# q, k and v of the second layer from four fp32r products in one PSUM bank, with a newly chosen order of all queues

## The reference

```
mod = silu(c) @ Wa + ba; sh_msa, sc_msa, g_msa, sh_mlp, sc_mlp, g_mlp = split(mod, 6)
h = layernorm(x) * (1 + sc_msa) + sh_msa
q, k, v = h @ Wq, h @ Wk, h @ Wv                  # 144 -> 3 x 144
w = softmax(q k^T / 3)                            # layer 1: causal; layer 0: full
x = x + g_msa * ((w v) @ Wp + bp)
h = layernorm(x) * (1 + sc_mlp) + sh_mlp
x = x + g_mlp * (act(h @ W1 + b1) @ W2 + b2)      # gelu in layer 0, silu in layer 1
```

## Time and profile before

| | |
|---|---|
| median of 3 runs | 292.33 us (292.04 to 294.12) |
| profiled execution | 292.45 us |
| its span, first to last instruction | 290.6 us |
| mean granted clock of TensorE | 0.988 |
| busy: TensorE, its weight loads, VectorE, ScalarE, GpSimd | 272.4, 157.0, 214.4, 198.2, 102.2 us |

### The profile page before, as it was taken

How to read it: one execution, slowest core, us unless ns; L and a number is a source line. 1 busy time by engine, 2 the same in 40 slices (tenths; PEclk the granted TensorE clock), 3 DMA queues, 4 the chain that set the end, 5 groups by cost and what they waited for, 6 DMA issues and landing times.

```text
span 290.6 us, 6567 instructions
## 1 busy us (share of the span) xinstructions
PE 272.4 (94%) x2418; PEld 157.0 (54%) x2418; DVE 214.4 (74%) x435; ACT 198.2 (68%) x357; POOL 102.2 (35%) x217
## 2 busy tenths in 40 slices
PE   8998889999999999999999989999799999899986
PEld 3685533434443634555636657665555455477576
DVE  7478999987677699996219997875655869943583
ACT  2163757778888698987884678476688776893271
POOL 6859084580005410001093120237824324311100
PEclk9998999999999999999999979999999999999999
DMA  5750000000000000000000000000000000001001
GB/s 144 215 139 1 2 0 0 3 0 2 0 2 0 2 0 2 2 2 0 0 2 2 0 2 2 2 0 3 0 2 2 2 1 2 3 0 33 10 2 42
DMA packets 5587, 4.60 MB, mean 16 GB/s; under 512 B 762, under 2 KB 5121, under 8 KB 5556
## 3 DMA queue, kind: packets, MB, share of 16 engines
q1 hardware_dynamic: 5556, 4.18, 5.2%
HBM read 3.59 MB, written 0.59 MB: 14 GB/s over the span
## 4 chain that ended last, share of the span: by engine, by line
PE 66%; DVE 15%; POOL 7%; issue 5%; ACT 5%; POOLq 0%; ACTq 0%; DVEq 0%
PE OB L1379 14%; DVE negm L1165 8%; PE banks L1358 7%; PE banks L1314 7%; PE banks L1331 7%; PE banks L1419 5%; PE banks L1286 3%; ACT probs L993 3%; PE banks L1287 2%; PE banks L1386 2%; PE banks L1216 2%; PE banks L1224 2%; POOL rowsT L876 2%; POOL rowsT L872 2%; PE banks L1277 2%
## 5 line engine op out<-in xcount | busy, mean ns | idle before, releaser
L1165 DVE TENSOR_REDUCE negm<-banks 128x2 f32<-128x1024 f32 (+2 forms) x112 | 124.4, 1141 | 29.2 <-PE banks L1342 19.1
L993 ACT ACTIVATE probs<-banks 128x1024 f32<-128x1024 f32 (+1 forms) x112 | 106.6, 966 | 27.6 <-PE banks L1358 25.4
L1379 PE MATMUL OB<-probs,V 128*10 128x512 f32 (+3 forms) x512 | 55.8, 515 | 0.4 <-POOL probs L906 0.4
L1331 PE MATMUL banks<-KS,QS 54*128 54x512 bf16 (+3 forms) x256 | 41.4, 346 | 2.7 <-DVE negm L1165 1.5
L1358 PE MATMUL banks<-QS,KS 56*128 56x512 bf16 (+3 forms) x256 | 39.5, 341 | 3.3 <-DVE negm L1165 1.2
L906 POOL TENSOR_SCALAR_AFFINE_SELECT probs<-probs 128x512 f32<-128x512 f32 x32 | 20.6, 646 | 54.4 <-ACT probs L993 54.4
L1314 PE MATMUL banks<-identb,rowsT 128*128 128x128 bf16 x384 | 29.7, 225 | 2.5 <-POOL rowsT L876 1.1
L1331 PEld LDWEIGHTS banks<-KS,QS 54*128 54x128 bf16 x256 | 11.8, 93 | 34.0 <-issue 11.9
L1314 PEld LDWEIGHTS banks<-identb,rowsT 128*128 128x128 bf16 x384 | 22.8, 100 | 12.2 <-issue 8.6
L1358 PEld LDWEIGHTS banks<-QS,KS 56*128 56x128 bf16 x256 | 10.9, 93 | 25.9 <-issue 12.3
L826 POOL TENSOR_TENSOR rstd<-veps,half 128x2 f32<-128x2 f32 (+1 forms) x14 | 10.4, 745 | 39.0 <-DVE veps L1095 38.9
(11 more groups left out here) (128 smaller groups left out, 463.1 us busy)
## 6 DMA issues: line engine op xcount, KB each, us to landing
X<-in_x SPq DMA_DIRECT2D x2, 288.0 KB, 3.3
out<-X SPq DMA_DIRECT2D x8, 72.0 KB, 1.6
xh<-in_L_cond_W_ada SPq DMA_DIRECT2D x2, 216.0 KB
xh<-in_L_cond_Wa SPq DMA_DIRECT2D x1, 432.0 KB
at<-in_L_cond_W_fc SPq DMA_DIRECT2D x1, 288.0 KB
xh<-in_L_cond_W SPq DMA_DIRECT2D x1, 288.0 KB
w_fc<-in_L_cond_W_fc SPq DMA_DIRECT2D x1, 288.0 KB
w_fc<-in_L_cond_W SPq DMA_DIRECT2D x1, 288.0 KB
```

Source lines behind the costliest of these rows:

```text
L993: nc.scalar.activation(e, s, ACT.Exp, scale=SCALE).then_inc(bank_free[BANK[item]], 1)
L1165: nc.vector.tensor_reduce(m, s, AX.X, ALU.max, negate=True).then_inc(bank_free[BANK[item]], 1)
L1331: ins = nc.tensor.matmul(o[:, i * w:(i + 1) * w], QS[b][rows, h // 2 + pair, qt * P:(qt + 1) * P], KS[b][rows, h // 2 + pair, 0:w], start= ...
L1379: ins = nc.tensor.matmul(OB[CT * j:CT * j + VW, q0:T], V[b][:, kt, h + j, :], probs[:, kt % 2, j, q0:T], start=(kt == 0), stop=(kt == NT - 1))
```

## The change

It has two parts.

In layer 1 (`WIDE = (1,)`) the items `qk` make q, k and v together: four fp32r products of 432 columns for one token tile, in one bank. For this hT is split on VectorE as for fc1 (the same hT_p and hT_s), the layer's q, k and v weights are split on chip by a new item `qsplit` (three copies on ScalarE, two subtractions on GpSimd, one more clearing on GpSimd in the opening), and ScalarE copies v out of the same bank before it rounds q and k. The items `v` of layer 1 go. Layer 0 keeps its fp32 products.

The order is another one: `HASTE`, `READING` and `CALM` have new values, and a table `NUDGE` adds a number to the precedence of 98 single steps. `WINDOW`, which was 0, goes.

```diff
+WIDE = (1,)
+def has_parts(l, k):
+    return k == 1 or l in WIDE
...
-WEIGHTS = ([("acol", 0, 1), ("agate", 0, 0), ("agate", 0, 1), ("wsplit", 0, 1), ("wsplit", 1, 1),
+WEIGHTS = ([("acol", 0, 1), ("agate", 0, 0), ("agate", 0, 1), ("wsplit", 0, 1), ("wsplit", 1, 1), *(("qsplit", l, 0) for l in WIDE),
...
-            if k:
+            if has_parts(l, k):
                 add("side", "DVE", item, (1600 if r else 1070) * size + 130 * (size < 1), ("ACT", item))
...
-OTHERS, CALM = 3, 4
-HASTE = {'head': (0, -1000, 27000, 0), 'tail': (3000, 8000, -3000, 0), 'gather': (-1000, 0, 15000, 0), 'shift': (0, 8000, 0, 0)}
+OTHERS, CALM = 3, 5
+HASTE = {'head': (-3000, 20000, 20000, 43000), 'tail': (4000, 31000, -3000, 0), 'gather': (-3000, 0, 3000, 1000),
+         'shift': (0, -1000, 23000, 0)}
...
-READING = {'weights': 5000, 'side': 300000, 'strips': 20000, 'shift': 60000, 'gather': 300000}
+READING = {'weights': 60000, 'side': 20000, 'strips': 20000, 'shift': 300000, 'gather': 300000}
...
+NUDGE = {('ACT', 'qT', (0, 0)): 6000, ('PE', 'sT', 15): 28500, ('DVE', 'proj', (1, 0)): 5500, ('DVE', 'max', 4): -4000,
...
+    first = {(q[0], item): urgency[q[0], item] + haste(q[1], item) + reading(q[0], q[1], item)
+             + NUDGE.get(of_what(q[0], item), 0) for q, items in queues.items() for item in items}
...
+            for l in range(L):
+                if l in WIDE:
+                    nc.gpsimd.memset(w_q_s[l][:, :].bitcast(F32), 0.0)
...
+        def q_pieces(l):
+            s, r = w_q_s[l], w_qkv_r[l][0:R, :]
+            return [(w_qkv[l][:, :], w_q[l][0][:, :], w_q[l][1][:, :]), (r, s[0:R, :], s[64:64 + R, :])]
...
+                elif kind == "qsplit":                                  # GpSimd
+                    l, _ = args
+                    pool.wait_ge(high_q[l], 1)
+                    (whole, high, low), (whole_r, high_r, low_r) = q_pieces(l)
+                    link(nc.gpsimd.tensor_tensor(low, whole, high.bitcast(F32), ALU.subtract))
+                    nc.gpsimd.tensor_tensor(low_r, whole_r, high_r.bitcast(F32), ALU.subtract).then_inc(low_q[l], 1)
+                    pool.wait_ge(low_q[l], 1)
...
+                elif kind == "qsplit":                                  # ScalarE
+                    l, _ = args
+                    act.wait_ge(qkv_in[l], 96 if l else 48)
+                    act.wait_ge(filled, 1)
+                    for whole, high, low in q_pieces(l):
+                        nc.scalar.activation(high, whole, ACT.Copy)
+                    nc.scalar.activation(w_q_s[l][32:32 + R, :], w_qkv_r[l][0:R, :], ACT.Copy).then_inc(high_q[l], 1)
...
                     if l:
                         full(act, ("sT", (b + 1) * NG - 1))
+                    if l in WIDE:
+                        attended(act, (b + 1) * NG - 1, NT - 1)
+                        nc.scalar.activation(V[b][:, t, :, 0:D],
+                                             bank_of(item)[:, QK:3 * C].rearrange("p (h d) -> p h d", h=H), ACT.Copy)
                     nc.scalar.activation(slots(b, t, slice(0, 2), HIGH, slice(0, H)),
...
                 elif kind == "qk":                                      # TensorE
                     l, b, t = args
+                    if l in WIDE:
+                        pe.wait_ge(low_q[l], 1)
+                        pe.wait_ge(split, HTN[("hT", l, b, 0, 0, part_with(l, b, 0, t))])
+                        tok = slice(t * P, (t + 1) * P)
+                        o = bank[:, 0:3 * C]
+                        nc.tensor.matmul(o, hT_p[0][:, tok], w_q[l][0][:, :], start=True, stop=False)
+                        nc.tensor.matmul(o, hT_p[0][:, tok], w_q[l][1][:, :], start=False, stop=False)
+                        nc.tensor.matmul(o, hT_p[1][:, tok], w_q[l][0][:, :], start=False, stop=False)
+                        nc.tensor.matmul(o, hT_s[:, tok], w_q_s[l][:, :], start=False, stop=True).then_inc(filled_bank, 1)
+                        continue
```

More of the change, by code:

```diff
@@ L77, in head_items @@
 def head_items(l, b):
-    after = ([("split", l, b, 0)] if (l, b) == (0, 0) else []) + [("v", l, b, i) for i in range(2)]
+    after = ([("split", l, b, 0)] if (l, b) == (0, 0) else []) + ([] if l in WIDE else [("v", l, b, i) for i in range(2)])
     qk = [("qk", l, b, t) for t in range(NT)]
@@ L204, in steps @@
             add(stream, "POOL", item, 2900, ("ACT", item))
+        elif kind == "qsplit":
+            add(stream, "ACT", item, 1430, 26000)
+            add(stream, "POOL", item, 2300, ("ACT", item))
         elif kind == "stats":
@@ L221, in steps @@
             if rows and rows != item[1:4]:
-                before = [("DVE", ("hT", *rows, 0, parts(*rows)[-1])) if rows[2] else ("PE", ("v", *rows[:2], 1))]
+                before = [("DVE", ("hT", *rows, 0, parts(*rows)[-1])) if rows[2] else ("PE", last_of_head(*rows[:2]))]
             if r == 0 and s != 1:
@@ L312 @@
 WORK = {"pv": 0.87, "acol": 0.03, "agate": 0.42, "max": 0.75, "scores": 0.8, "hT": 0.62, "aT": 0.62}
-WINDOW = 0
 def reader_of(item):
@@ L336, in mode, with of_what @@
+def of_what(engine, item):
+    return engine, item[0], item[1] if item[0] in ("max", "scores", "msplit", "sT", "pv", "oT", "o", "tri") else item[1:3]
 def mode(item):
@@ L424, in plan @@
                     start = max(start, at_best)
-                mine_best.append((start, -urgency[engine, item] - haste(stream, item) - reading(engine, stream, item) - (STICK if engine == "PE" and mode(item) == last else 0), engine, stream, item, k))
+                mine_best.append((start, -first[engine, item] - (STICK if engine == "PE" and mode(item) == last else 0), engine, stream, item, k))
             if mine_best:
-                first = min(mine_best)[0]
-                chosen = min((c for c in mine_best if c[0] <= first + WINDOW), key=lambda c: c[1])
+                chosen = min(mine_best)
                 if best is None or chosen[0] < best[0]:
@@ L524, in two_block_kernel @@
         w_qkv_r = [sb(f"w_qkv_r{l}", [SR, 3 * C]) for l in range(L)]
+        w_q = {l: [sb(f"w_q{l}{i}", [P, 3 * C], F32R) for i in range(2)] for l in WIDE}
+        w_q_s = {l: sb(f"w_q_s{l}", [SR, 3 * C], F32R) for l in WIDE}
         w_fc1 = [[sb(f"w_fc1{l}{i}", [P, FF], F32R) for i in range(2)] for l in range(L)]
@@ L625, in two_block_kernel @@
         tri_ready = sem("tri_ready")
+        high_q = {l: sem(f"high_q{l}") for l in WIDE}
+        low_q = {l: sem(f"low_q{l}") for l in WIDE}
         pv_done = sem("pv_done")
@@ L643, in two_block_kernel @@
         GATE = ordinals(("gate",))
-        HTN = {item: n for n, item in enumerate((i for i in SIDE if i[0] == "hT" and i[3]), 1)}
+        HTN = {item: n for n, item in enumerate((i for i in SIDE if i[0] == "hT" and has_parts(i[1], i[3])), 1)}
         NORM_SETS = list(dict.fromkeys(i[1:4] for i in SIDE if i[0] == "norm"))
@@ L706, in rows_used @@
             else:
-                full(eng, ("v", l0, b0, 1))
+                full(eng, last_of_head(l0, b0))
         block = ctx.enter_context(nc.Block())
@@ L1375, in _ @@
                     if kt % 2 == 0 and g % NG == 0:
-                        released(pe, ("v", l, b, kt // 2))
+                        for t in range(kt, kt + 2):
+                            released(pe, v_from(l, b, t))
                     q0 = first_query(l, kt)
```

36 lines of the change are left out of this document (33 added, 3 removed), and 8 rows, old and new, of the table NUDGE.

## The result

The changed kernel takes 301.75 us (median of 4 runs, 301.54 to 305.3), the kernel before on the same chip 293.23 (4 runs). The ratio is 1.0325, with a 95% interval of 1.0281 to 1.0369: slower by 3.3%, where 285.3 was forecast with a range up to 293.5.

A forecast was written before the change was run, and what follows sets the result against it. TensorE was taken as the bound, with batch 1's layer-1 projection a latency in front of GpSimd. 292.45 - 5.7 (products) - 1.4 (order, chain cost recovered) = 285.3 us; range 278.5 to 293.5.

The forecast's parts named there:

- The port: Eight new two-input VectorE subtractions can hold GpSimd's selects about 0.3 us each; counted 0, bound +1 us.
- The order: New queue orders start batch 1's layer-1 head earlier, recover its chain cost and close a TensorE hole: -1.4 us.
- The products: TensorE, layer 1's q, k, v: 16 fp32r products a batch at 0.19 us replace 5.90 us of fp32; gain 5.7 us.
- Splitting hT: Layer 1's heads: five more VectorE instructions per half set, 7.2 us; batch 0 free, +1.1 us on batch 1's chain.
- Rival C: VectorE becomes the bound at layer seams and heads, where splits queue among reductions: 296 to 299.7 us, chance 0.13.
- Rival D: The wide product on TensorE takes four passes, not one: 304.3 us, chance 0.02.
- ScalarE: Four V copies of 144 columns a batch, near 0.24 us each, replace two: +0.1 us a batch, hidden outside batch 1's chain.
- Rounding the weights: Layer 1's weight split on ScalarE and GpSimd plus a GpSimd clearing in the opening: cost zero, 0.45 if a reader waits.

The follow-up runs named there:

- experiment 1: The changed kernel, but GpSimd begins gating batch 1's layer-0 weights only when VectorE's norm of batch 1 is done: 293.27 us, ratio to before 1.0012.
- Experiments 9 to 12: Wide products in before's order, 302.93 us; two fp32 products instead, 308.86; experiment 1 with first-half splits earlier, 296.08; with batch 1's second half earlier, 295.76.
- the exact old order: The kernel before with its order kept item by item and only layer 1's wide products, their hT splits and the weight split put in: 302.93 us, 1.0302.
- the fp32 twin: The kernel of the exact old order, with two fp32 products of 432 columns in place of the four fp32r, still waiting for the splits: 308.86 us, 1.0529.

## Why the prediction was wrong

**The port** is the step that failed. It priced the collision of VectorE and GpSimd for the eight new two-input subtractions against GpSimd's selects, at 0 with a bound of +1. For GpSimd that was right: the longest select after is 697 ns, 928 before. But the added instructions were held themselves. In the head of batch 1 in experiment 1 two of the first five start just after a select and take 0.70 and 0.85 us, where they take 0.28 and 0.42 otherwise:

```profile
190.09 0.64 POOL L992 TENSOR_SCALAR_AFFINE_SELECT probs<-probs 128x512 f32<-128x512 f32 x1 [1.17 <-ACT probs L1091]
190.16 0.70 DVE L1217 CAST hT_s<-hT_r 16x256 fp32r<-16x256 f32 x1
191.91 0.64 POOL L992 TENSOR_SCALAR_AFFINE_SELECT probs<-probs 128x512 f32<-128x512 f32 x1 [1.19 <-ACT probs L1091]
191.97 0.85 DVE L1223 TENSOR_TENSOR hT_p<-hT,hT_p 128x256 fp32r<-128x256 f32 x1
```

The trace of before had this direction too, beside the one of the earlier trace rows:

```profile
250.51 0.64 POOL L906 TENSOR_SCALAR_AFFINE_SELECT probs<-probs 128x512 f32<-128x512 f32 x1 [0.29 <-ACT probs L993]
250.53 0.77 DVE L1124 CAST hT_p<-hT 128x256 fp32r<-128x256 f32 x1
```

And the price asked only what the *added* instructions would meet. The order had moved old instructions: GpSimd's gating and weight split of batch 1 now stood beside a norm with one input, which nothing in the diff touches. There too VectorE waits, and the hold lasts for the series, not for an instruction: 5.3 us, 8.5 with what followed. The rule that I drew on (the Trainium skill, "SBUF — State Buffer", section "SBUF: two separate sides") names this pair too, a VectorE instruction in a mode with two ports against a GpSimd one; that the norm ran in that mode no run shows. The runs agree that the two exclude each other, and show a length that I did not price.

**The order**, priced at -1.4 us with +1.7 and new waits at worst, failed likewise. The stretch at half clock was on my list (+1.7), but the one that came was longer (0.52 and 0.50 over the 9 us from 36 to 45, in two kernels with the same hole); filling the hole gave back 3.3. And order and products don't add up. Wide products cost 9.7 us in the old order and the order 6.8 with the old products, both against before; together they cost 0.2 (293.27 - 293.12). The new order seems to fit the longer heads: it gets batch 1's second norm done at the same time (190.1 against 190.7), and with a head 4.5 us longer group 11's maxima are still at 206.9 in both. Why it does so was not tested step by step.

**The products** was right in mechanism and size: 0.20 us a product (0.19 taken), TensorE 5.3 us less busy (5.7), 6.5 and 5.9 us less time in two pairs of kernels that differ in them alone.

**Splitting hT** was mis-sized. The five instructions take what was said (0.28 to 0.42 us) when no select is beside them, but I took +1.1 us for batch 1's chain and nothing for batch 0, as if they ran as soon as hT was there. In experiment 1 ScalarE's hT is ready at 188.4 us, the splits start at 190.16, behind two row maxima and the second half's norm, and the first product at 192.97. Of these 2.81 us (190.16 to 192.97) 0.85 are the two holds above. In batch 0's head the first half waits likewise (hT ready at 133.35, splits at 135.72). The second half's splits start at once, at 195.94 and 140.67, but its transposes stand behind the products of the first. Measured from norm to qk: +3.1 us in batch 0 (9.7 against 6.6) and +4.5 in batch 1 (10.8 against 6.3).

**Rival C** said that splits queue among the reductions and that VectorE's shortage turns TensorE's gain into idle time. Experiments 9 to 12 show it in these orders. Its place (the heads, 188 to 206 us) was right; its price, 3.6 to 7.2 us above before, was low for the old order (9.7, though the products gained 6). In the new order the products did bring their gain (6.5 us), and the order's own 6.8 cancelled it; how much of that is room made for the longer heads no run separates. **Rival D** is out, 0.20 us a product. **ScalarE**: a V copy of 144 columns took 0.29 us (0.24 taken). **Rounding the weights**: GpSimd still idles 2.17 us ahead of the first rstd, as forecast. In the exact old order the opening was 2.2 us late (1.5 in the fp32 twin), with TensorE's clock at 0.64 (0.70) in 36 to 45 us, while `qsplit` stood among ScalarE's first items; I did not try it elsewhere, so that cause is only argued.

Without the collision the time would have been just inside the range (293.27 against 293.5), and that would have been luck, with the gain missing all the same. Two errors of one sign stand behind the difference of 16.5 us: 8.5 for the collision, and 8.0 for heads and order (293.27 - 285.3).

## What to carry to other kernels

When a change reorders queues, list for every long unbroken GpSimd series which VectorE instructions from SBUF to SBUF now fall beside it, old ones first, and let the series wait for those that TensorE needs. A cheaper product that needs a step on another engine is worth its gain only where that step is not queued: read the queue of that engine between the source and the product, not the step's duration. Test order and content apart, in all four combinations, since each may be slower alone and neutral together.

## What the runs showed of the hardware

- A VectorE tensor_scalar from SBUF to SBUF that met a back-to-back series on GpSimd was held until the first gap in it, 0.07 to 0.08 us, for 5.31, 5.96, 5.91, 5.90, 5.95 and 2.37 us in six kernels. A row maximum, which reads PSUM, took its usual 1.23 us beside the same series (at 27.58 us in after). With one select of 0.64 us beside them, casts and subtractions of hT took 0.32 to 0.48 us longer. The wait shows as the instruction's own duration; an engine that looks full (8.00 of 8 us with six instructions) may be held. GpSimd lost nothing: five gatings took 2.26 us beside it and 2.27 before.
- The second norm instruction then took 1.54 us beside L962 (1.39 us), the last two 0.34: it was held once more by the one that followed the gap.
- After TensorE had idled 5.09 us the granted clock averaged 0.61 from 36 to 45 us, with TensorE busy 8.83 of these 9; in a second kernel 0.52, busy 7.85, and 1.00 from 45 us on. Being full did not bring 2.4 GHz back at once. With the hole filled the same stretch had 1.00. In the profiled execution of after the clock fell a second time, 0.72 in 55 to 70 us with TensorE busy 14.72 of 15, and no run shows why.
- An fp32r product of 432 columns starts 0.20 us after the one before at full clock and 0.36 at half; its weight load, 0.19 us at full clock and 0.33 at half, lies beside the product before.
